# A decoder layer on one core: query stacks read part by part from a scratch in the stack's order, the residual sum as its own GpSimd step, and a new step order

## The chip, the cores and the metric

The kernel runs on one core of a Trainium2 chip. TensorE (PE) multiplies matrices into the eight banks of PSUM, VectorE (DVE) and ScalarE (ACT) read PSUM and SBUF, GpSimd (POOL) works on SBUF, and SyncE (SP) issues every DMA here. The metric is the device time of one execution in microseconds, the median of three runs.

## What is computed

One decoder layer on x (4 batches, 512 rows, 128 features), all in float32:

```
x = x + attn(layernorm(x))        # self attention by distances: softmax(-gamma * |xi - xj|^2) @ x
x = x + xattn(layernorm(x), ctx)  # 16 heads of 8 features over 154 context rows, with ALiBi slopes
x = x + ffn(layernorm(x))         # 8 experts of 128x128, the two best of each row, no weighting

scores = einsum('bhqd,bhkd->bhqk', q, k) / sqrt(dk) + slopes * (i - j)
attn   = softmax(scores, axis=-1)
```

## The kernel before

Each of the four batches b goes through the same steps. A step is written `name:b` or `name:b.k`, and each engine walks its own list of them in `ORDER` (line 44 on). The five lists are fixed tables, so an engine that meets a step whose semaphore is not yet there waits, and everything behind it in its list waits too. The tables stand for SP ("sync"), POOL ("gpsimd"), ACT ("scalar"), DVE ("vector") and PE ("tensor").

The steps of a batch in the order of the data:

- `stats1`, `rstd1`, `y1`, `y1T`: first layernorm (DVE statistics, POOL square root at L459, DVE normalising at L670) and its transpose through PE and ACT.
- `dist`, `rowmax`, `soft`, `probs`, `self`: distances as 512x512 matmuls (L913), row maxima on DVE (L687, L700), exponentials on ACT (L559), transposes of them, and the attention sum on PE (L932).
- `gather` (DVE, L710) adds the input and gives x1, with the statistics of the second layernorm; `rstd2` (POOL, L457 and L459), `y2` (DVE, L670), `y2T`.
- `query`: a matmul (L945), ACT's scaled copy into `qf` (L587), and a split into three bf16 parts `qpart`: the first by ACT, the second and third by DVE (L757 to L761). SP writes the parts to `q_scratch` in DRAM and reads them back as the stack `qs`, in which each head's 8 features stand six times in the order that the bf16 products need (`Q_PART`, 48 rows for each parity s of the head). Before the change SP waits for all three writes and then reads 48 rows of 8 pieces of 1 KB for each s. The key stacks `kA` and `kB` are made alike from `k_scratch`, once for each batch.
- `maxima` (PE L973, DVE L768): the largest score of each row and head, 22 groups of up to three heads through the two banks `MX`. It needs `qs` and `kA`. `mcat`, `mT`: the 64 maxima of a row, transposed, go through `m_scratch` in DRAM into six rows of `qs`.
- `scores` (PE L999 and L1003, ACT exponentials L611) needs `kB` and those six rows; `values` (L1019, L1023), `divide`, `aoT`, `wo` (L1050), with x2 from DVE (L801).
- x1 plus the output bias is `x1b`, which `wo` adds. It is made on POOL at the end of `rstd2` (L521), right behind the square root.
- `y3`, `y3T`, `route` (L1061), `mask`, then for each expert `spread` (PE L1083), `select` (DVE L848), `experts` (PE L1096); `fT`, `store`.

`WARM` (L117) puts matmuls on constant data (L870) ahead of certain steps; they compute nothing that is used. There are 91 of them in the program. Keys are prepared in the first batch: `keys:0` is two ACT copies (L572), four DVE instructions (L732 to L738), and DMAs that SP issues.

## Time and profile before

| | |
|---|---|
| median of 3 runs | 244.94 us (243.94 to 246.68) |
| the profiled execution | 244.3 us |
| its span | 242.5 us |
| PE matmuls busy | 206.0 us, 85% |
| DVE busy | 157.9 us, 65% |
| ACT busy | 109.2 us, 45% |
| POOL busy | 36.7 us, 15% |
| DMA traffic | 16.91 MB |

The span runs from the first to the last instruction; the time of the execution has 1.8 us more around it. Matmul busy time counts the matmuls on constant data as well, and a busy share is a mean over stages with different limits, so the stages are read one by one.

### The profile page before, as it was taken

The page shows a single profiled execution, that of the slowest core. Times are in us where ns is not written, and L with a number is a line of the kernel's source. Part 1 is how long each engine was busy: PE and PEld are TensorE (multiplying, and loading weights), DVE is VectorE, ACT ScalarE, POOL GpSimd, SP SyncE. Part 2 cuts the span into 40 slices and gives each one's busy share as a digit, 9 for nine tenths or more (in the row PEclk, how much of TensorE's full clock was granted, in tenths as well). Part 3 has the DMA queues.
Part 4 walks back from the last instruction along what each step waited for, and adds up shares of the span by engine and source line. Part 5 has one row for each costly group of instructions (what it writes and reads, how often), then busy time and mean ns, then how long its engine had stood idle before and what let it go on. Part 6 is the DMA issues. An engine that isn't in the chain of part 4 may idle for free.

```text
span 242.5 us, 3528 instructions
## 1 busy us (share of the span) xinstructions
PE 206.0 (85%) x1206; PEld 104.7 (43%) x1224; DVE 157.9 (65%) x433; ACT 109.2 (45%) x206; POOL 36.7 (15%) x98
## 2 busy tenths in 40 slices
PE   7488956878958898998999999889987878899994
PEld 2247622436612234474353457643333342335573
DVE  2476536499662488847686699776589513479772
ACT  2286053730317476828635566276133137821300
POOL 5604184300130030005000000130000001002000
PEclk9999999999975999999999999999999979999999
DMA  6997504900204500120152021203601010000011
GB/s 170 310 265 259 110 1 158 223 4 0 57 0 144 119 1 0 41 59 0 68 142 53 0 45 43 58 3 131 130 0 40 11 51 0 0 4 0 1 46 43
DMA packets 23031, 16.91 MB, mean 70 GB/s; under 512 B 10548, under 2 KB 21644, under 8 KB 22924
## 3 DMA queue, kind: packets, MB, share of 16 engines
q1 hardware_dynamic: 23012, 16.67, 26.8%
q8 instruction: 10, 0.16, 0.3%
q14 instruction: 9, 0.07, 0.1%
HBM read 11.29 MB, written 5.37 MB: 69 GB/s over the span
## 4 chain that ended last, share of the span: by engine, by line
PE 50%; DVE 24%; ACT 9%; issue 7%; POOL 4%; DMA 3%; another core or an unknown queue 1%; SPq 0%; ACTq 0%; DVEq 0%; POOLq 0%
DVE nm L768 12%; PE bank L1096 11%; PE bank L875 6%; PE bank L932 5%; PE bank L1023 4%; PE bank L913 4%; PE bank L973 3%; PE bank L1083 3%; DVE y L670 3%; PE bank L1003 3%; POOL rs L459 3%; PE bank L1019 2%; PE bank L870 2%; ACT w L551 2%; DVE x L710 2%
## 5 line engine op out<-in xcount | busy, mean ns | idle before, releaser
L768 DVE TENSOR_REDUCE nm<-bank 128x3 f32<-128x462 f32 x88 | 49.4, 618 | 10.9 <-PE bank L973 10.7
L611 ACT ACTIVATE pt<-bank 128x512 f32<-128x512 f32 x64 | 34.7, 597 | 22.9 <-PE bank L1003 15.2
L973 PE MATMUL bank<-kA,qs 128*128 128x308 bf16 (+1 forms) x172 | 29.2, 264 | 6.5 <-DVE nm L768 5.3
L1096 PE MATMUL bank<-ym,ewT 128*128 128x512 f32 (+1 forms) x80 | 32.5, 511 | 0.3 <-DVE ym L848 0.3
L848 DVE TENSOR_TENSOR ym<-bank,y3T 128x512 f32<-128x512 f32 (+1 forms) x40 | 22.1, 579 | 8.2 <-PE bank L1083 6.8
L870 PE MATMUL bank<-idle 128*128 128x512 bf16 x82 | 22.9, 406 | 3.3 <-DVE idle L655 1.5
L457 POOL TENSOR_SCALAR ve<-mv 128x4 f32<-128x4 f32 (+1 forms) x13 | 2.6, 198 | 151.4 <-DVE mv L663 151.1
L973 PEld LDWEIGHTS bank<-kA,qs 128*128 128x128 bf16 x172 | 12.1, 97 | 28.5 <-DVE nm L768 24.0
L1003 PE MATMUL bank<-qs,kB 128*128 128x512 bf16 x59 | 20.5, 397 | 3.4 <-ACT ptail L611 1.2
L913 PE MATMUL bank<-y1Tg,y1T 128*128 128x512 f32 x32 | 17.9, 641 | 5.5 <-ACT w L551 4.4
L551 ACT ACTIVATE w<-bank,snsq,sgn 128x512 f32<-128x512 f32 x16 | 12.3, 773 | 16.0 <-DVE rm L687 16.0
L687 DVE TENSOR_REDUCE rm<-bank 128x1 f32<-128x512 f32 x16 | 10.9, 688 | 12.6 <-PE bank L914 12.6
L1023 PE MATMUL bank<-pt,vm 128*32 128x512 f32 x128 | 16.9, 598 | 0.3 <-issue 0.3
L670 DVE TENSOR_SCALAR y<-x,mv,rs 128x128 f32<-128x128 f32 x32 | 11.3, 425 | 8.1 <-POOL rs L459 8.0
L1096 PEld LDWEIGHTS bank<-ym,ewT 128*128 128x128 f32 x80 | 13.6, 190 | 5.1 <-DVE ym L848 1.8
L932 PE MATMUL bank<-y,pT 128*128 128x128 f32 x128 | 15.3, 278 | 0.2 <-ACT pT L535 0.2
L870 PEld LDWEIGHTS bank<-idle 128*128 128x128 bf16 x91 | 8.9, 102 | 14.8 <-issue 2.4
L932 PEld LDWEIGHTS bank<-y,pT 128*128 128x128 f32 x128 | 14.6, 192 | 0.6 <-ACT pT L535 0.4
L875 PE MATMUL bank<-ident,y 128*128 128x128 f32 x48 | 7.7, 280 | 6.9 <-DVE y L670 6.9
L559 ACT ACTIVATE w<-w,nrb,sgn 128x512 f32<-128x512 f32 x16 | 12.9, 811 | 1.0 <-DVE nrb L700 0.6
L459 POOL TENSOR_TENSOR rs<-ve,minus_half 128x4 f32<-128x4 f32 (+1 forms) x13 | 13.2, 1012 | 1.1
L1003 PEld LDWEIGHTS bank<-qs,kB 128*128 128x128 bf16 x64 | 6.2, 101 | 14.1 <-ACT pt L611 7.4
(130 smaller groups left out, 275.3 us busy)
## 6 DMA issues: line engine op xcount, KB each, us to landing
qs<-q_scratch SPq DMA_DIRECT2D x8, 384.0 KB, 4.9
q_scratch<-qpart SPq DMA_DIRECT2D x4, 384.0 KB, 2.4
xs<-in_x_dram SPq DMA_DIRECT2D x4, 256.0 KB, 7.2
vm<-in_vm_ones_dram SPq DMA_DIRECT2D x1, 1024.0 KB, 12.0
q_scratch<-qpart SPq DMA_DIRECT2D x4, 256.0 KB, 2.1
kA<-k_scratch SPq DMA_DIRECT2D x8, 120.0 KB, 2.7
kB<-k_scratch SPq DMA_DIRECT2D x8, 120.0 KB, 2.6
out_dram<-ob SPq DMA_DIRECT2D x3, 256.0 KB, 2.4
```

The source lines that it names most:

```text
L459: g.tensor_tensor(rs[:, at], ve[:, at], minus_half[:, at], ALU.pow).then_inc(rstd[i], 1)
L611: nc.scalar.activation(dst, ST[n % 2][:, :], ACT.Exp).then_inc(exps, 1)
L768: v.tensor_reduce(negated[:, GROUP * g:GROUP * g + heads], MX[n % 2][:, 0:heads * J].rearrange("p (s j) -> p s j", s=heads), AX.X, ALU.max ...
L848: v.tensor_tensor(ym[:, e, at], MX[n % 2][:, at], y3T[:, at], ALU.mult).then_inc(mx_free, 1)
L870: mm(bank_[:, :], idle[:, 0:P], idle[:, :], start=True, stop=True)
L875: last = nc.tensor.transpose(bank_[:, tile(t)], src(t), id_[:, :])
L913: mm((A0S, A1S)[t % 2][b][:, :], y1T[:, tile(t)], y1Tg[:, :], start=True, stop=False)
L932: last = mm(A0S[b][:, tile(t)], pT[:, b % 2, t, u, :], y1[:, b % 2, u, :], start=(u == 0), stop=(u == T - 1))
L973: last = mm(MX[n % 2][:, at * J:(at + heads) * J], qs[:, b % 2, a, tile(t)], kA[:, s:s + heads, a, 0:J], start=True, stop=True)
L1003: last = mm(ST[n % 2][:, :], kB[:, h % 2, h // 2, 0:JM], qs[:, b % 2, h // 2, :], start=True, stop=True)
L1023: last = mm(YV[32 * g:32 * g + 32, :], vm[:, b, R * g + k, :], pt[:, (G * k + g) % PT_RING, :], start=False, stop=(k % 2 == 1), skip_group ...
L1096: last = mm(YMS[b][p][:, at], ewT[:, e, :], ym[:, e, at], start=False, stop=(e == E - 1))
```

## The change

Four things are edited.

1. The rows of Wq and Wk are permuted on the way in (`order`), so that a partition of q and k is (parity s, feature c, pair a). The scratches become `[2, COPY, HALF, ...]`, laid out as the stacks are. A row of a stack is then one contiguous piece (8 KB for `qs`, 2,560 bytes for a key stack).
2. Each write of a part is two DMAs of 64 partitions instead of one of 128, each part has a semaphore of its own, and `qs` is read in six DMAs (24, 16 and 8 rows for each s), each pair behind its own part's write. Key writes are twice as many DMAs as well.
3. `x1b` becomes a step `residual` that waits for the third part of the query (`q_lo`) and stands at another place in POOL's list.
4. All five lists of `ORDER` are replaced, and so is `WARM`: 63 matmuls on constant data instead of 91.

```diff
-        k_scratch = nc.dram_tensor("k_scratch", [B, P, COPY, JP], BF16, kind="Internal").ap()
-        q_scratch = nc.dram_tensor("q_scratch", [P, COPY, S], BF16, kind="Internal").ap()
+        k_scratch = nc.dram_tensor("k_scratch", [B, 2, COPY, HALF, JP], BF16, kind="Internal").ap()
+        q_scratch = nc.dram_tensor("q_scratch", [2, COPY, HALF, S], BF16, kind="Internal").ap()
...
             def query(b, _):
+                if b >= 1:
+                    sp.wait_ge(qs_in, 6 * ONE * b)
                 for part, (got, (r, n)) in enumerate(zip((q_hi, q_mid, q_lo), RUNS)):
                     sp.wait_ge(got, b + 1)
-                    load(q_scratch[:, r:r + n, :], qpart[:, part, :].unsqueeze(1).broadcast_to([P, n, S]), q_out)
+                    for s in range(2):
+                        load(q_scratch[s, r:r + n].rearrange("k p n -> p k n"),
+                             qpart[s * HALF:(s + 1) * HALF, part, :].unsqueeze(1).broadcast_to([HALF, n, S]), q_out[part])
...
-                sp.wait_ge(q_out, 3 * ONE * (b + 1))
-                for s in range(2):
-                    load(qs[s * ROWS:(s + 1) * ROWS, b % 2, :, :],
-                         q_scratch.rearrange("(a s c) k n -> s (c k) a n", s=2, c=DK)[s], qs_in)
+                for part, (r, n) in enumerate(RUNS):
+                    sp.wait_ge(q_out[part], 2 * ONE * (b + 1))
+                    for s in range(2):
+                        load(qs[s * ROWS + r * DK:s * ROWS + (r + n) * DK, b % 2, :, :],
+                             q_scratch[s, r:r + n].rearrange("k (c a) n -> (k c) a n", c=DK), qs_in)
...
             def rstd2(b, _):
                 norm(1, b, mv2, ve2, rs2)
+
+            def residual(b, _):
+                pool.wait_ge(q_lo, b + 1)
                 if b == 0:
                     pool.wait_ge(weights_in, W_LOADS * ONE)
...
-    order = np.arange(D)
+    order = np.arange(D).reshape(PAIRS, 2, DK).transpose(1, 2, 0).reshape(D)
```

The list of POOL and the constants of `WARM`, before and after:

```diff
-        rstd1:0 rstd1:1 rstd2:0 weights:0 rstd1:2 rstd2:1 rstd1:3 rstd2:2 rstd3:0 rstd3:1 rstd2:3 rstd3:2
-        rstd3:3.0 rstd3:3.1
+        rstd1:0 rstd1:1 rstd2:0 weights:0 rstd1:2 residual:0 rstd2:1 rstd1:3 residual:1 rstd3:0 rstd2:2 rstd3:1
+        residual:2 rstd2:3 residual:3 rstd3:2 rstd3:3.0 rstd3:3.1
...
-    "y1T:0": 14, "probs:0": 1, "y1T:1": 9, "y2T:0": 9, "query:0": 2, "probs:1": 16, "maxima:0": 1, "y2T:1": 16,
-    "query:1": 2, "scores:0": 1, "scores:1": 2, "y2T:2": 3, "wo:1.0": 1, "y3T:1.0": 2, "scores:2": 2, "y2T:3": 2,
-    "query:3": 1, "maxima:3": 1, "divide:2.1": 3, "spread:3.0": 3,
+    "y1T:0": 16, "probs:0": 1, "y2T:0": 10, "query:0": 1, "probs:1": 6, "y1T:2": 6, "y2T:1": 5, "query:1": 4,
+    "scores:0": 2, "divide:0.1": 2, "scores:1": 1, "scores:2": 6, "spread:3.0": 3,
```

The lines of the file shift by up to 11, so a row of before at L973 stands at L984 in the changed kernel. Three places show what moves.

DVE in the first batch, from the second layernorm of batch 0 (`y<-x`) to the first maxima (`nm<-bank`), before:

```order
L670 TENSOR_SCALAR y<-x,mv,rs 128x128 x4
L757 TENSOR_TENSOR qr<-qf,qpart 128x512
L759 CAST qpart<-qr 128x512
L761 TENSOR_TENSOR qpart<-qr,qpart 128x512
L687 TENSOR_REDUCE rm<-bank 128x1 x4
L670 TENSOR_SCALAR y<-xs,mv,rs 128x128 x4
L697 SCALAR_TENSOR_TENSOR rma<-rm,sgn,snsq 128x4
L700 TENSOR_SCALAR nrb<-rma,nsgn 128x4
L768 TENSOR_REDUCE nm<-bank 128x3 x21
```

and now:

```order
L681 TENSOR_SCALAR y<-x,mv,rs 128x128 x4
L768 TENSOR_TENSOR qr<-qf,qpart 128x512
L770 CAST qpart<-qr 128x512
L772 TENSOR_TENSOR qpart<-qr,qpart 128x512
L698 TENSOR_REDUCE rm<-bank 128x1 x4
L708 SCALAR_TENSOR_TENSOR rma<-rm,sgn,snsq 128x4
L711 TENSOR_SCALAR nrb<-rma,nsgn 128x4
L681 TENSOR_SCALAR y<-xs,mv,rs 128x128 x4
L779 TENSOR_REDUCE nm<-bank 128x3 x21
```

The first layernorm of batch 2 (`y<-xs`) has moved from ahead of the row maxima of batch 1 (`rma`, `nrb`) to behind them.

PE just ahead of the maxima of the last batch (`kA,qs`), with the last experts of batch 1 (`ym,ewT`), its scores (`qs,kB`) and values (`pt,vm`) of batch 2, before:

```order
L1003 MATMUL bank<-qs,kB 128x512 x2
L1083 MATMUL bank<-maskT,spread 128x512
L1023 MATMUL bank<-pt,vm 32x512 x4
L1096 MATMUL bank<-ym,ewT 128x512 x2
L870 MATMUL bank<-idle 128x512
L973 MATMUL bank<-kA,qs 128x308
L973 MATMUL bank<-kA,qs 128x154 x2
L973 MATMUL bank<-kA,qs 128x308
L1096 MATMUL bank<-ym,ewT 128x512
```

and now:

```order
L1107 MATMUL bank<-ym,ewT 128x512 x2
L1094 MATMUL bank<-maskT,spread 128x512
L1014 MATMUL bank<-qs,kB 128x512 x2
L1107 MATMUL bank<-ym,ewT 128x512
L984 MATMUL bank<-kA,qs 128x308
L984 MATMUL bank<-kA,qs 128x154 x2
L984 MATMUL bank<-kA,qs 128x308
L1034 MATMUL bank<-pt,vm 32x512 x4
L984 MATMUL bank<-kA,qs 128x308
```

The second half of the values, `values:2.1`, now stands behind the first maxima, and of the experts two (`experts:1.6` and `1.7`) stand behind the last of them, where `mT:3` follows.

SP around the query of batch 1, before:

```order
L346 DMA qs<-m_scratch 6x4096
L346 DMA q_scratch<-qpart 128x3x512
L346 DMA q_scratch<-qpart 128x2x512
L346 DMA q_scratch<-qpart 128x512
L346 DMA qs<-q_scratch 48x8x512 x2
L346 DMA kB<-k_scratch 48x8x160 x2
```

and now:

```order
L346 DMA qs<-m_scratch 6x4096
L346 DMA q_scratch<-qpart 64x3x512 x2
L346 DMA q_scratch<-qpart 64x2x512 x2
L346 DMA q_scratch<-qpart 64x512 x2
L346 DMA qs<-q_scratch 24x4096 x2
L346 DMA qs<-q_scratch 16x4096 x2
L346 DMA qs<-q_scratch 8x4096 x2
L346 DMA kB<-k_scratch 48x1280 x2
```

Twelve DMAs take the place of five, and a read's row is 4096 elements in one piece.

## Rows read from the trace of the kernel before

**Rows 1.** Page: busy us, share, count of each engine; TensorE's clock, 40 slices.
```profile
PE 206.0 (85%) x1206; PEld 104.7 (43%) x1224; DVE 157.9 (65%) x433; ACT 109.2 (45%) x206; POOL 36.7 (15%) x98
PEclk9999999999975999999999999999999979999999
```
**Rows 2.** Stretches: length, busy us of PE, PEld, DVE, ACT, POOL; clock, DMA, GB/s.
```profile
59.00:84.30 25.30, 20.70 (x97) 9.30 (x102) 13.03 (x49) 10.22 (x18) 3.59 (x5) 0.80 0.30 76
107.00:131.50 24.50, 21.95 (x118) 9.77 (x120) 17.78 (x50) 13.72 (x25) 3.48 (x5) 1.00 0.30 74
131.50:155.30 23.80, 23.29 (x163) 14.72 (x164) 19.34 (x48) 13.32 (x26) 1.20 (x2) 1.00 0.11 28
155.30:176.00 20.70, 18.76 (x99) 7.72 (x101) 13.50 (x35) 10.38 (x19) 2.26 (x3) 1.00 0.37 88
176.00:188.40 12.40, 10.14 (x61) 4.35 (x64) 11.72 (x21) 4.23 (x8) 0.00 (x0) 1.00 0.09 20
188.40:196.20 7.80, 5.67 (x47) 2.26 (x50) 3.49 (x11) 1.78 (x3) 0.00 (x0) 0.98 0.18 48
```
**Rows 3.** The same of L870 alone, the matmuls on constant data (PE, weight loads).
```profile
107.00:131.50 24.50, 1.19 (x4) 0.49 (x5) 1.00 0.30 74
155.30:176.00 20.70, 1.84 (x6) 0.58 (x6) 1.00 0.37 88
188.40:196.20 7.80, 0.59 (x2) 0.21 (x3) 0.98 0.18 48
```
**Rows 4.** Timeline of DVE: start, us, operation [idle before, releaser].
```profile
30.48 2.05 DVE L670 TENSOR_SCALAR y<-x,mv,rs 128x128 f32<-128x128 f32 x4 [1.50 <-POOL rs L459]
37.99 0.69 DVE L761 TENSOR_TENSOR qpart<-qr,qpart 128x512 bf16<-128x512 f32 x1
43.21 1.11 DVE L670 TENSOR_SCALAR y<-xs,mv,rs 128x128 f32<-128x128 f32 x4
...
66.83 1.82 DVE L670 TENSOR_SCALAR y<-x,mv,rs 128x128 f32<-128x128 f32 x4 [1.50 <-POOL rs L459]
```
**Rows 5.** Timeline of POOL at the first residual sum.
```profile
30.34 1.09 POOL L521 TENSOR_TENSOR x1b<-x,cols 128x512 f32<-128x512 f32 x1
```
**Rows 6.** Timeline of ACT: key copies, and around the exponentials of batch 1.
```profile
19.39 0.90 ACT L572 ACTIVATE kf<-bank,cols 128x308 f32<-128x308 f32 x2
...
43.33 0.78 ACT L551 ACTIVATE w<-bank,snsq,sgn 128x512 f32<-128x512 f32 x1 [0.30 <-DVE rm L687]
44.75 0.81 ACT L559 ACTIVATE w<-w,nrb,sgn 128x512 f32<-128x512 f32 x1 [0.64 <-DVE nrb L700]
```
**Rows 7.** Chain that ended last, in order of time: start, us, what.
```profile
47.60 10.19 DVE nm L768 x18
...
179.04 9.07 DVE nm L768 x16
...
191.24 2.04 DMA m_scratch<-mT
193.30 2.54 DMA qs<-m_scratch
```
**Rows 8.** Timeline of SP: the issues of the first query, writes and reads.
```profile
36.69 2.36 SPq L346 DMA_DIRECT2D q_scratch<-qpart  x3
40.48 0.83 SPq L346 DMA_DIRECT2D qs<-q_scratch  x2
```
**Rows 9.** DMAs from 36 to 50 us: landing of qs's reads; third write.
```profile
DMA to landing us min/median/max: 4.6/5.1/5.6
...
q_scratch<-qpart SPq DMA_DIRECT2D x1, 128.0 KB, 1.7
```
**Rows 10.** PE in the stretch at the lower clock.
```profile
69.00:80.00 11.00, 9.32 (x32) 2.43 (x31) 3.58 (x13) 6.26 (x11) 0.27 (x1) 0.53 0.36 107
```
**Rows 11.** Timeline of PE: the first matmuls behind two waits of about 2 us.
```profile
40.15 1.12 PE L913 MATMUL bank<-y1Tg,y1T 128*128 128x512 f32 x2 [2.25 <-ACT w L551]
...
68.71 0.66 PE L875 MATMUL bank<-ident,y 128*128 128x128 f32 x4 [2.02 <-DVE y L670]
```

More of the change, by code:

```diff
@@ L62 @@
[L62 to L65 removed]
+        y1T:0 dist:0.0 dist:0.1 soft:0.0 soft:0.1 dist:0.2 soft:0.2 dist:0.3 soft:0.3 probs:0.0 probs:0.1
+        probs:0.2 keys:0 probs:0.3 y1T:1 y2T:0 query:0 dist:1 soft:1.0 soft:1.1 probs:1.0 probs:1.1 soft:1.2
@@ L91 @@
-        scores:0.7 maxima:1.7 scores:0.8 maxima:1.8 divide:0.0 scores:0.9 maxima:1.9 values:0.2 maxima:1.10
-        values:0.3 probs:2.2 probs:2.3 divide:0.1 mT:1 self:2 aoT:0 scores:1.0 wo:0 scores:1.1 scores:1.2
-        scores:1.3 y2T:2 scores:1.4 y3T:0 query:2 route:0 scores:1.5 values:1.0 mask:0 values:1.1 spread:0.0
-        spread:0.1 y1T:3 spread:0.2 experts:0.0 spread:0.3 spread:0.4 experts:0.1 spread:0.5 experts:0.2
-        spread:0.6 spread:0.7 dist:3 maxima:2.0 experts:0.3 experts:0.4 maxima:2.1 scores:1.6 experts:0.5
@@ new lines @@
+        maxima:0.7 probs:1.3 maxima:0.8 maxima:0.9 maxima:0.10 self:1 y1T:2 mT:0 y2T:1 query:1 scores:0.0
+        scores:0.1 scores:0.2 scores:0.3 dist:2 scores:0.4 maxima:1.0 values:0.0 maxima:1.1 scores:0.5
+        maxima:1.2 scores:0.6 maxima:1.3 probs:2.0 scores:0.7 maxima:1.4 values:0.1 maxima:1.5 scores:0.8
+        maxima:1.6 divide:0.0 maxima:1.7 probs:2.1 scores:0.9 maxima:1.8 values:0.2 maxima:1.9 values:0.3
+        maxima:1.10 divide:0.1 probs:2.2 probs:2.3 aoT:0 mT:1 wo:0 self:2 scores:1.0 y3T:0 scores:1.1 route:0
@@ new lines @@
+        scores:1.2 scores:1.3 values:1.0 mask:0 y2T:2 scores:1.4 spread:0.0 spread:0.1 query:2 spread:0.2
+        scores:1.5 spread:0.3 experts:0.0 experts:0.1 spread:0.4 spread:0.5 y1T:3 experts:0.2 experts:0.3
+        spread:0.6 spread:0.7 dist:3 maxima:2.0 experts:0.4 experts:0.5 maxima:2.1 experts:0.6 experts:0.7
+        maxima:2.2 scores:1.6 fT:0 maxima:2.3 scores:1.7 values:1.1 maxima:2.4 scores:1.8 divide:1.0 maxima:2.5
+        scores:1.9 values:1.2 maxima:2.6 values:1.3 maxima:2.7 probs:3.0 divide:1.1 probs:3.1 maxima:2.8 aoT:1
@@ new lines @@
+        probs:3.2 maxima:2.9 wo:1 maxima:2.10 probs:3.3 self:3 mT:2 y3T:1 route:1 scores:2.0 mask:1 y2T:3
+        scores:2.1 spread:1.0 query:3 spread:1.1 spread:1.2 experts:1.0 scores:2.2 spread:1.3 experts:1.1
+        scores:2.3 experts:1.2 spread:1.4 spread:1.5 values:2.0 spread:1.6 scores:2.4 experts:1.3 experts:1.4
+        spread:1.7 scores:2.5 experts:1.5 maxima:3.0 values:2.1 maxima:3.1 scores:2.6 maxima:3.2 maxima:3.3
+        scores:2.7 maxima:3.4 maxima:3.5 maxima:3.6 scores:2.8 maxima:3.7 maxima:3.8 maxima:3.9 scores:2.9
@@ L584, in query @@
                 if b >= 1:
-                    act.wait_ge(q_out, 3 * ONE * b)
+                    for part in range(3):
+                        act.wait_ge(q_out[part], 2 * ONE * b)
                     act.wait_ge(q_lo, b)
```

103 lines of the change are left out of this document (47 added, 56 removed).

## The prediction, made before the changed kernel ran

> **What bounds the kernel now.** I read the page first, then the chain that ended last, then the engines' busy time in stretches between the steps, and last the timelines where an engine waits. The page [rows 1] shows matmuls on PE for 85% of the span, constant ones (L870) among them, and the clock line shows two weak places. The chain [rows 7] says what the page cannot: for 10.19 us behind 47.60 and 9.07 us behind 179.04 it lies on DVE's maxima (L768), near the end on the round trip of the maxima through DRAM, and elsewhere mostly on PE. So there are three kinds of stretches. From 131.5 to 155.3 PE is busy 23.29 of 23.80 us [rows 2]: there an order can gain almost nothing. From 176 to 188.4 DVE sets the pace. And ahead of the first maxima (26 to 47.6 us), from 59 to 84.3, and from 155.3 to 196.2, the path runs through a single batch's chain (normalise, query, DRAM, maxima), with PE waiting or running constant matmuls. That is where this change can act.
>
> **The DRAM round trip of the query.** In the first batch the third part is ready at 38.68 (37.99 + 0.69) [rows 4]. SP's issues of the writes end at 39.05, the third lands after 1.7 us [rows 9], the reads go out from 40.48 in 0.83 us for two [rows 8], and the later lands 5.6 us after its issue at about 40.8 [rows 9], so at 46.4: 7.7 us behind the third part. Now SP issues eight DMAs behind the third part (two writes, six reads) at 0.42 us each, by the pair of reads. The last issue starts 7 x 0.42 = 2.9 us behind it; the first two parts are already in DRAM by then. For the landing of the last read, of 64 KB in 8 KB rows, the nearest row is the read of `m_scratch`, which has 8 KB rows too, 2.54 us [rows 7]; the other end is today's 5.6 us. I take 2.6, since the last pair carries a sixth of the bytes: 5.5 us in all, against 7.7, and 8.5 at the worst end. The trip is 2.2 us shorter, or 0.8 longer.
>
> The Trainium skill ("DMA: Bandwidth & Descriptors", section "Why a DMA increments its semaphore by 16 and not by 1") says that a DMA runs on the largest number of engines up to 16 that divides its slowest dimension: 24, 16 and 8 rows would get 12, 16 and 8 engines where 48 rows have 16. By that the trip would shorten less or not at all. No row here shows the number of engines of a DMA.
>
> **Up to the first maxima, 3.2 us.** (a) The two key copies on ACT, 0.90 us at 19.39 [rows 6], stood ahead of all four copies of the first probabilities; three of these now go first. The attention sum can start after three, so it starts about 0.7 us earlier. Nothing takes this back: the key parts on DVE end about 2 us later than now, and their DMAs have until the maxima. (b) y2 takes 2.05 us while x1b (L521) runs beside it on POOL from 30.34, and 1.82 us in batch 1, where the same four instructions take 1.11 us with POOL idle [rows 4, 5, 6]. x1b now comes later, but in this batch POOL's `weights` follows in its place; I count 0.5 of the 0.94. (c) ACT's copies of y1T now come before those of y2T instead of between y2T and the query's copy: 0.3. So the third part is ready 1.5 us earlier, at 37.2. (d) The first exponential of batch 1 started at 44.75 and waited 0.64 us for DVE [rows 6], which had 1.11 us of y1:2 in front of the row maxima [rows 4]; that is now behind them. The relu copies end at 44.1 - 1.5 = 42.6 and the exponential follows at once, to 43.4. Transposes (0.45) and the first group bring the maxima to 44.4 instead of 47.6 [rows 7]: 3.2 us. The stack lands at 37.2 + 5.5 = 42.7, in time; at the worst end it lands at 45.7 and 1.5 us of the gain are lost. Ten fewer constant matmuls at probs:1 cost nothing: they filled this wait.
>
> **The second query, 0.4 us.** y2:1 gains 0.7 of its 1.82, but mT now stands ahead of y1T:2 on ACT, and with three copies behind it y2T:1 starts 0.3 late. The values' bias sums (2.3 us on DVE) move from behind y2:1 to ahead of gather:1, where the attention sum is still running.
>
> **The middle, 84.3 to 155.3, 1.0 us.** Idle time and constant matmuls are 24.50 - 21.95 + 1.19 = 3.7 us from 107 to 131.5, and about 0.7 from 131.5 to 155.3 [rows 2, 3]. The stack of batch 1 lands well ahead of its maxima. Every order has the same useful matmuls here, so between 0 and 3.7 can be won; I take 1.0, since the new order fills some waits with experts but pushes `self:2` behind `wo:0`.
>
> **From 155.3 to 196.2, 3.2 us.** Idle time and constant matmuls are 3.8 + 2.3 + 2.7 = 8.8 of 40.9 us (each length less busy plus L870's share) [rows 2, 3]; useful are 32.1. The stack of batch 3, 2.2 us earlier, lets the maxima start earlier, and the order fits: two experts and `values:2.1` (1.7 and 0.9 us) go behind the first maxima. What stays: six constant matmuls (1.3), unfilled waits (1.0), waits inside the maxima, where 22 groups at 9.07/16 = 0.57 us are a floor of 12.5 (1.5), and the wait for the maxima's trip, 2.04 + 2.54 us [rows 7], less what PE has to do meanwhile (1.8). That is 5.6 instead of 8.8 us. Here lies a new cost too: residual:2 follows rstd3:1 on POOL, so x1b runs beside y3:1 instead of y2:3, which moves 0.7 us and saves none in that batch. `stats1:3` now waits on SP ahead of the kB loads of batch 2; they come later than now, behind the last maxima of batch 2, but still ahead of mT:2's trip, which the scores need as well, so at no cost.
>
> The Trainium skill ("SBUF — State Buffer", section "Who interferes with whom") says that the port pair of VectorE and GpSimd is an exclusive lock for a whole instruction, against VectorE's two-port modes, and never against a reduction. By that the later x1b is free beside the maxima of batches 0 and 1 and costs the 0.7 us beside y3:1.
>
> **The rest, 0.4 us.** Two constant matmuls and a small wait ahead of the last values. The tail behind 216 us keeps its work.
>
> **Sum:** 3.2 + 0.4 + 1.0 + 3.2 + 0.4 = 8.2 us off the profiled execution's 244.3: 236.1. The median of the runs shown is 0.6 above that execution, so 236.7; I say 236.5. The terms' ends are 1.7 to 3.7, 0 to 1, 0 to 3.7, 0.5 to 4.5 and 0 to 1.
>
> **Rivals.** (1) *The gain of the front is not passed on*: a wait in the crowded lists of the later batches, or one more stretch at the lower clock, takes back the last three terms. Left are 3.2 + 0.4: 241. For it speaks the stretch at 131.5, where PE has no slack; against it the 8.8 us further on. (2) *The trip gets no shorter*, since twelve issues replace five and a read of 8 rows cannot use the whole DMA side: 0.8 us lost ahead of the first maxima and 1.8 in batch 3: 5.6 left, 239. This is the rival of the skill's rule on engines. (3) *The clock stays full.* From 69 to 80 us it was granted at 0.53 of 2.4 GHz, so for nearly all of it at its lower level of 1.2 GHz, after PE had been idle for 2.02 us [rows 11] and busy only in pieces, with 9.32 us of matmuls [rows 10]; I put what the full level would save at a third of these, 3 us, since matmuls double in their columns alone. If PE gets through there, 233.5. (4) *Slower*: the 28 constant matmuls that are gone held the clock. If PE falls to 1.2 GHz in the waits of all three other queries and of mT:3 too, at 3 us each, 12 us are lost and 8.2 won: 248.5. It decides from three such stretches beyond today's; one costs only rival 1. Against it speaks that a wait of 2.25 us at 40.15 [rows 11] left the clock line at its nines [rows 1], and that the new order shortens those waits.
>
> **How the numbers follow.** Chances: forecast 0.50 (its own range 234 to 239), rival 1 0.20, rival 2 0.12, rival 3 0.12, rival 4 0.06. The range from 232.0 to 241.5 leaves out rival 4, part of rival 1, and a full clock together with full terms. A measurement of this kernel tells 1% (2.4 us) from no change. Above 242.5 lie a third of rival 1 and a little of rival 2, within 1%; above 247.4 most of rival 4. Faster 0.86, same 0.09, slower 0.05.
>
> **What would show it.** The first group of maxima at 44 to 45 us; the reads of qs landed within 6 us of the third part; y2 of batches 1 and 3 at 1.1 us and y3:1 at 1.8; the maxima of the last batch starting at about 168 us instead of 176, and the scores of batch 3 at 188 to 189 instead of 196. I am wrong if the reads land later than 8 us after the third part, if PE's clock line shows more than two weak places, or if PE idles longer behind 84 us than now.

## The result and the profile after

The change made the kernel slower: 257.8 us (median of 4 runs, 256.54 to 258.4) against 245.69 us (243.94 to 246.68) before, a ratio of 1.049 [1.042, 1.057]. I had forecast 236.5 us and given "slower" 5 in 100. The profiled execution took 257.5 us with a span of 255.7 us. All ratios in this document, with their 95% intervals in brackets, leave out executions that were over 1.5% longer than the fastest of their kernel, at a lower granted clock; the medians take all.

The page of the changed kernel, PE's busy line and the clock line, answers [rows 1]:

```profile
PE 208.2 (81%) x1181; PEld 107.3 (42%) x1196; DVE 157.4 (62%) x433; ACT 109.9 (43%) x206; POOL 35.2 (14%) x98
...
PEclk9999999675999889997998899959988999999999
```

PE is busy for 2.2 us more although 28 constant matmuls are gone, and the clock line, with two weak places before, now has weak places in every part of the program. The reason stands in the chain that ended last (start, us, what), here its steps on the query's reads, on the last maxima and on their trip:

```profile
40.70 6.38 DMA qs<-q_scratch
...
81.96 6.35 DMA qs<-q_scratch
...
133.42 6.13 DMA qs<-q_scratch
...
183.37 5.63 DMA qs<-q_scratch
...
193.52 9.08 DVE nm L779 x16
...
207.21 2.64 DMA qs<-m_scratch
```

Before, the chain of [rows 7] had DVE's maxima at 179.04. They now stand at 193.52, as fast as then (9.08 against 9.07 us), and in all four batches the chain runs through the reads that the change was to shorten. Next the timelines of the changed kernel: DVE with y2 and the third part of the first batch, SP with its issues of writes and reads, and PE with the first group of maxima of each batch:

```profile
29.26 1.27 DVE L681 TENSOR_SCALAR y<-x,mv,rs 128x128 f32<-128x128 f32 x4 [0.33 <-POOL rs L466]
...
35.92 0.69 DVE L772 TENSOR_TENSOR qpart<-qr,qpart 128x512 bf16<-128x512 f32 x1
```
```profile
34.46 3.98 SPq L346 DMA_DIRECT2D q_scratch<-qpart  x6
38.54 2.45 SPq L346 DMA_DIRECT2D qs<-q_scratch  x6
```
```profile
47.22 0.93 PE L984 MATMUL bank<-kA,qs 128*128 128x308 bf16 x4 [3.67 <-DMA qs<-q_scratch]
...
88.55 0.93 PE L984 MATMUL bank<-kA,qs 128*128 128x308 bf16 x4 [3.20 <-DMA qs<-q_scratch]
...
139.80 0.93 PE L984 MATMUL bank<-kA,qs 128*128 128x308 bf16 x4 [3.50 <-DMA qs<-q_scratch]
...
189.34 0.56 PE L984 MATMUL bank<-kA,qs 128*128 128x308 bf16 x4 [3.74 <-DMA qs<-q_scratch]
```

The third part is ready at 36.61 (35.92 + 0.69), 2.1 us earlier than in [rows 4]. The maxima start at 47.22, when PE started them at 47.20 before. I call the time from the third part to the first maxima the trip: it takes 10.6 us, 10.5 of them to the landing of the reads (40.70 + 6.38 = 47.08), where [rows 8, 9] gave 7.7 to the landing. PE stands idle for over 3 us in each batch, and in three batches of four the first four matmuls behind that wait take 0.93 us, in the last 0.56. The stretches of the changed kernel (columns as in [rows 2]), from the start of one batch's maxima on:

```profile
47.20:66.70 19.50, 16.78 (x87) 11.08 (x89) 14.85 (x35) 3.38 (x7) 0.00 (x0) 0.66 0.14 34
...
139.80:163.50 23.70, 23.57 (x162) 14.57 (x163) 17.94 (x42) 12.29 (x24) 1.91 (x3) 0.94 0.01 3
163.50:189.90 26.40, 20.71 (x102) 9.40 (x106) 14.52 (x41) 10.00 (x18) 2.64 (x4) 0.87 0.32 81
189.90:203.00 13.10, 10.60 (x55) 4.02 (x57) 11.69 (x21) 4.69 (x9) 0.00 (x0) 0.87 0.00 0
```

From 47.2 to 66.7 the granted clock is 0.66 of 2.4 GHz, between its two levels and so for most of the stretch at 1.2 GHz. The three last stretches, at 0.94, 0.87 and 0.87, answer those of [rows 2] that stood at 1.00.

### The profile page after: what moved, and what is told of

It reads as the page before. It is cut to its first block, busy times and chain, and to the rows that moved or that the text cites. A ratio compares the mean times of both kernels' runs of the same rounds, so it can differ in the third digit from the quotient of the medians.

```text
span 255.7 us, 3526 instructions
## 1 busy us (share of the span) xinstructions
PE 208.2 (81%) x1181; PEld 107.3 (42%) x1196; DVE 157.4 (62%) x433; ACT 109.9 (43%) x206; POOL 35.2 (14%) x98
## 4 chain that ended last, share of the span: by engine, by line
PE 42%; DVE 19%; DMA 14%; ACT 8%; SPq 8%; issue 6%; POOL 2%; ACTq 0%; DVEq 0%; POOLq 0%
DMA qs<-q_scratch 10%; DVE nm L779 8%; SPq L346 8%; PE bank L886 7%; PE bank L984 6%; PE bank L1107 6%; PE bank L1034 5%; PE bank L943 3%; PE bank L1030 3%; PE bank L1014 3%; DVE ym L859 2%; DVE y L681 2%; PE bank L956 2%; PE bank L1072 2%; DVE st L671 1%
## 5 line engine op out<-in xcount | busy, mean ns | idle before, releaser
L984 PE MATMUL bank<-kA,qs 128*128 128x308 bf16 (+1 forms) x172 | 32.4, 298 | 20.0 <-DMA qs<-q_scratch 14.1
L984 PEld LDWEIGHTS bank<-kA,qs 128*128 128x128 bf16 x172 | 13.9, 106 | 45.1 <-DVE nm L779 24.6
L1014 PE MATMUL bank<-qs,kB 128*128 128x512 bf16 x57 | 19.2, 394 | 3.4 <-ACT pt L622 1.8
L924 PE MATMUL bank<-y1Tg,y1T 128*128 128x512 f32 x32 | 16.9, 610 | 5.2 <-ACT w L561 4.4
L881 PE MATMUL bank<-idle 128*128 128x512 bf16 x57 | 17.4, 448 | 3.2 <-DVE idle L666 1.5
L1034 PE MATMUL bank<-pt,vm 128*32 128x512 f32 x128 | 18.0, 637 | 0.0
L698 DVE TENSOR_REDUCE rm<-bank 128x1 f32<-128x512 f32 x16 | 10.9, 689 | 10.4 <-PE bank L925 10.4
L943 PEld LDWEIGHTS bank<-y,pT 128*128 128x128 f32 x128 | 15.6, 203 | 0.4 <-ACT pT L545 0.4
L545 ACT ACTIVATE pT<-bank 128x512 f32<-128x512 f32 x16 | 9.3, 595 | 15.1 <-PE bank L886 15.1
L622 ACT ACTIVATE ptail<-bank 128x512 f32<-128x512 f32 x16 | 8.7, 596 | 11.9 <-PE bank L1010 11.9
L886 PE MATMUL bank<-ident,w 128*128 128x128 f32 x64 | 10.7, 304 | 1.1 <-ACT pT L545 0.5
```

The costliest lines, as they stand in the source:

```text
L622: nc.scalar.activation(dst, ST[n % 2][:, :], ACT.Exp).then_inc(exps, 1)
L881: mm(bank_[:, :], idle[:, 0:P], idle[:, :], start=True, stop=True)
L886: last = nc.tensor.transpose(bank_[:, tile(t)], src(t), id_[:, :])
L924: mm((A0S, A1S)[t % 2][b][:, :], y1T[:, tile(t)], y1Tg[:, :], start=True, stop=False)
L943: last = mm(A0S[b][:, tile(t)], pT[:, b % 2, t, u, :], y1[:, b % 2, u, :], start=(u == 0), stop=(u == T - 1))
L984: last = mm(MX[n % 2][:, at * J:(at + heads) * J], qs[:, b % 2, a, tile(t)], kA[:, s:s + heads, a, 0:J], start=True, stop=True)
```

## The experiments

Three theories stood against each other at first: the new reads are slow because 24, 16 and 8 rows get few DMA engines (A); they are slow because of their 8 KB rows (B); the new order itself costs, with 28 fewer constant matmuls, and the trip only shows it (C). Each experiment ran beside runs of the kernel before, whose medians were 243.6 to 244.4 us. The ratios below are to these.

**The order alone.** Kernel before, its DMAs and layout untouched, with the `residual` step, `ORDER` and `WARM` of the changed kernel.

> The kernel before with all of its DMAs, scratch layouts and permutation, but with the residual step, the five lists and the constants of the changed one. Theories A and B (the trip is what costs): the trip is 7 to 8 us again, the maxima of batch 0 start near 45 us, and the time is 238 to 244 us, my forecast without its shorter trip (239) being in it. Theory C (the order, with 28 fewer constant matmuls, costs): 250 us or more, with weak places in the clock line although the trip is short.

**237.6 us**, ratio 0.974 [0.964, 0.984]: faster by 6.7 us, and theory C falls. Its page, and the starts of its first and last maxima and of the scores of batch 3 on PE:

```profile
PE 197.0 (84%) x1196; PEld 100.7 (43%) x1196; DVE 156.5 (67%) x433; ACT 109.7 (47%) x206; POOL 35.9 (15%) x98
...
PEclk9999999999999999999999999999999999999999
```
```profile
44.18 0.56 PE L975 MATMUL bank<-kA,qs 128*128 128x308 bf16 x4 [0.92 <-DMA qs<-q_scratch]
...
168.56 0.56 PE L975 MATMUL bank<-kA,qs 128*128 128x308 bf16 x4 [0.52 <-DMA qs<-q_scratch]
...
187.97 0.61 PE L1001 MATMUL bank<-qs,kB 128*32 128x512 bf16 x8 [0.94 <-DMA qs<-m_scratch]
```

In this execution the same lists with the same 63 constant matmuls hold PE's clock at full level throughout, with a trip of 7.8 us (36.34 to 44.18). PE is busy 11.2 us less than in the changed kernel for the same work. This execution was the fastest of e3's four (235.4 us); the other three took 237.6 to 237.9 us at a mean clock of 0.983 to 0.986. The same kernel with DMAs behind its end (e12) had its clock low for about 10 us between 48 and 62 us. So the full clock is the best case of e3, and not assured by its order.

**The DMAs alone.** Changed kernel with the lists, `WARM` and the place of `x1b` from before.

> The changed scratches, permutation, writes and six reads, but the lists, the constants and the place of x1b of the kernel before. Theories A and B: the trip is 10.5 to 11 us instead of 7.7, the maxima start about 3 us late in each of four batches, and the time is 251 to 257. Theory C: 244 to 248, as before, since the longer trip is hidden.

251.5 us, ratio 1.032 [1.021, 1.043]; the trip in batch 0 is 10.3 us (40.35 to 50.63). So the new DMAs cost 7 us in the old order and 20 us in the new one (257.8 less 237.6). The new order is worth 6.7 us with the short trip and costs 6 with the long one: the two parts of the change are not additive.

**Two reads instead of six, and 1 KB pieces instead of 8 KB rows.** Both on the changed kernel.

```diff
# e1_two_reads, behind the writes of all three parts
+                for s in range(2):
+                    load(qs[s * ROWS:(s + 1) * ROWS, b % 2, :, :],
+                         q_scratch[s].rearrange("k (c a) n -> (k c) a n", c=DK), qs_in)
# e2_pieces
+        q_scratch = nc.dram_tensor("q_scratch", [2, COPY, HALF, S + 32], BF16, kind="Internal").ap()[:, :, :, 0:S]
```

> The changed kernel, but qs is read by one DMA of 48 rows for each s (two instead of six), behind the writes of all three parts. Rows stay 8 KB in one piece; lists, constants and writes stay those of the changed kernel, in which the maxima started 10.6 to 11.3 us behind the third part and always waited last for the reads. Theory A (reads of 24, 16 and 8 rows have too few DMA engines): the trip falls to 8 us or less, the clock's weak places ahead of and behind the maxima shrink, and 257.8 us falls by 8 to 12, to 246 to 250. Theory B (the contiguous 8 KB rows are what is slow, on however many engines): the trip stays within 1 us of 10.6 and the time at 255 to 258. Theory C (the new order is to blame, the trip only shows it): 255 to 258 too, with a shorter trip.

> The changed kernel, but each 512-element line of q_scratch is followed by 32 unused elements, so a row of qs is again 8 pieces of 1 KB; the six reads, writes, lists and constants stay. Theory A (few engines for 24, 16 and 8 rows): the same bytes on as few engines, trip 10 to 12 us, time 256 to 260. Theory B (8 KB pieces are slow): trip 8 us or less, time 246 to 250. If both were at work, a trip in between.

Two reads: 249.2 us, ratio 1.025 [1.014, 1.037], trip 9.5 us. Pieces: 256.4 us, ratio 1.049 [1.036, 1.063], trip 10.9 us. Row size makes no difference that shows (256.4 against 257.8 us, 10.9 against 10.6), and the split of the reads does. But the two reads leave 1.7 us of the longer trip, which my text had not named.

**Sixteen rows for each read, and whole writes.** To get writes of 128 partitions with 8 KB rows, the scratch was laid out as copy, partition, column.

```diff
# e5_sixteen_rows
+                for k, part in ((0, 0), (2, 1), (4, 2)):
+                    sp.wait_ge(q_out[part], 2 * ONE * (b + 1))
+                    for s in range(2):
+                        load(qs[s * ROWS + k * DK:s * ROWS + (k + 2) * DK, b % 2, :, :],
+                             q_scratch[s, k:k + 2].rearrange("k (c a) n -> (k c) a n", c=DK), qs_in)
# e8_three_writes (two reads) and e9_three_writes_sixteen (the six reads of e5)
+        q_scratch = nc.dram_tensor("q_scratch", [COPY, P, S], BF16, kind="Internal").ap()
...
+                         q_scratch[:, s * HALF:(s + 1) * HALF].rearrange("k (c a) n -> k c (a n)", c=DK), qs_in)
```

> The changed kernel, still with six reads and six writes, but the reads take 16 rows each (copies 0 and 1, 2 and 3, 4 and 5 of the stack, behind parts 1, 2 and 3) instead of 24, 16 and 8. Theory A (24 and 8 rows use too few DMA engines, 16 rows use all): no read is on few engines, so the rate while they run rises from about 125 GB/s to 190 to 270, and although the last pair now carries a third of the bytes, the maxima start 8 to 9.5 us behind the third part instead of 10.6 to 11.3; time 247 to 251, about that of the two reads of 48 rows (249.2) or better. Theory A' (what costs is six small reads behind one another, whatever their rows): trip 10.5 to 11.5, time 255 to 259.

> The two reads of 48 rows (249.2 us), and the scratch laid out as copy, partition, column, so that each part is again one write of 128 partitions: five issues instead of eight, rows still 8 KB in one piece. Theory D (what is left of the longer trip after the repair of the reads is the twelve, here eight, issues on SP, of which the pairs of writes cost 1.5 us): reads issued 1.5 us earlier, trip 7.7 to 8.2, time 240 to 244. Theory B (8 KB pieces have a price of their own): trip 9 us or more and 246 to 249.

> Both repairs, and still part by part: three writes of 128 partitions and six reads of 16 rows, each pair behind its part. If theories A and D hold, this is the trip that the change was written for: a third of the bytes behind the last part, 6 to 7.5 us, maxima of batch 0 at 43 to 44 us, time 235 to 240. If part-by-part reading gains nothing on this path, 240 to 246, no better than the two reads.

255.2 us (1.046 [1.040, 1.051]), 257.6 us (1.059 [1.054, 1.064]) and 287.6 us (1.181 [1.177, 1.186]). e5 came out as theory A' said: no read has fewer than 16 rows, and the trip is still 10.5 us, so theory A in its simple form does not carry the loss. The times of e8 and e9 missed every value that I had written down. In e8 and e9 I had changed more than I meant to: the outermost dimension of a read's source is now the copy, of size 6 and 2. First of e8, then of e9: the chain's step on the first batch's reads (start, us), and the DMA lines (GB/s in 40 slices, for e9 also the busy tenths of the 16 engines) of a later batch's reads, from 82 to 91 us and from 144 to 163 us:

```profile
40.20 8.18 DMA qs<-q_scratch
```
```profile
GB/s 73 146 0 36 109 146 146 109 182 73 109 146 109 146 182 36 109 73 109 109 182 146 109 218 146 146 109 146 73 73 36 0 0 0 0 0 0 0 0 0
```
```profile
40.23 14.12 DMA qs<-q_scratch
```
```profile
DMA  0002001011111111111111011111111111110000
GB/s 26 17 0 34 0 34 52 34 52 52 52 52 69 52 52 52 52 52 52 52 52 69 34 69 52 52 52 52 52 52 52 52 69 52 52 52 0 0 0 0
```

With an outer dimension of 2 the reads run at a nearly even 52 GB/s with 10 to 20% of the 16 engines' time busy; if that is two engines, each moves 26 GB/s. With 6 the slices lie mostly between 73 and 182. That is the rule of the Trainium skill ("DMA: Bandwidth & Descriptors", section "Why a DMA increments its semaphore by 16 and not by 1"), that the slowest dimension sets the number of engines, and here the trace agrees. A limit of 2 or 6 engines is met in these two kernels alone.

**Constants into the waits.** Ten constant matmuls ahead of the maxima of each batch in the changed kernel; six, four, six and six in the kernel with two reads.

```diff
# e6_constants; e14_two_reads_constants has 6, 4, 6, 6
+    "maxima:0": 10, "maxima:1": 10, "maxima:2": 10, "maxima:3": 10,
```

> The changed kernel with ten more matmuls on constant data ahead of the maxima of every batch, into the wait of 3.2 to 3.7 us for the reads (ten take about 3 us at the full clock), so the reads are as late as in the changed kernel but PE does not stand idle for them. Theory E (a large part of the loss is the clock that falls behind each wait, PE being busy 208.2 us where the same list takes 197.0 at the full clock): 249 to 253, a granted clock of 0.97 or more, the groups of maxima of batch 0 in 12.4 us instead of 15.1. If the clock costs little beside the waits themselves: 255 to 258.

> The two reads of 48 rows (249.2 us, trip 9.5 to 10.4) with six, four, six and six matmuls on constant data in the waits ahead of the maxima. By theory E the clock's share of what is left is recovered: the waits of 1.7 to 3.3 us stay as they are, but the clock line keeps its nines, 241 to 245. If the remaining loss is only late data: 247 to 249.

250.2 us (1.025 [1.018, 1.032]) and 245.1 us (1.003 [0.999, 1.008]), so 7.6 us come back against the changed kernel and 4.1 against the kernel with two reads, although the data arrives hardly sooner: the trips in e6 are 10.5 to 10.9 us, and the four of e14 take 38.8 us where e1's took 39.9. The stretch of the maxima of batch 0, changed kernel and then e6 (columns as in [rows 2]):

```profile
47.20:57.00 9.80, 7.83 (x38) 4.31 (x38) 7.80 (x14) 2.78 (x6) 0.00 (x0) 0.67 0.19 40
```
```profile
49.80:59.00 9.20, 6.68 (x46) 3.50 (x46) 8.83 (x16) 2.78 (x6) 0.00 (x0) 1.00 0.22 47
```

46 matmuls take 6.68 us at the full clock, 38 take 7.83 at 0.67; the maxima's own take 265 ns each in the one and 341 in the other.

**A longer trip and nothing else.** The new order with the old DMAs (e3), plus one DMA of 1 KB and its wait between the query's writes and reads.

```diff
# e10_longer_trip
+                load(pause[b], qpart[0:16, 2, 0:32], paused)
+                sp.wait_ge(paused, ONE * (b + 1))
```

> The kernel with the new order and the old DMAs (237.6 us), and one small DMA of 1 KB with its wait put between the query's writes and its reads on SP: the trip grows by about 2.3 us (0.4 to issue, 1.7 to 2 to land), to 10.1 us from 7.8, near the 10.6 to 11.3 of the changed kernel, and nothing else changes. Theory F (the length of the trip alone, with the clock that falls in the longer waits, explains the changed kernel's loss of 20 us): well over 4 x 2.3 = 9.2 us, at 249 to 256, with several weak places in the clock line. If the waits cost only their length: 245 to 247. If something else in the changed DMAs (keys, 64-partition writes beside other work) is at fault: 240 to 244, the rest being hidden.

248.1 us, ratio 1.017 [1.012, 1.023]: 10.4 us lost against e3. SP's rows, PE's first maxima, and the seven us from about the start of the maxima of batches 0 and 1 on (columns as in [rows 2]):

```profile
38.31 0.33 SPq L346 DMA_DIRECT2D pause<-qpart  x1
39.63 0.83 SPq L346 DMA_DIRECT2D qs<-q_scratch  x2
```
```profile
45.42 0.55 PE L979 MATMUL bank<-kA,qs 128*128 128x308 bf16 x4 [1.98 <-DMA qs<-q_scratch]
```
```profile
45.00:52.00 7.00, 5.31 (x29) 2.94 (x30) 5.39 (x10) 2.78 (x6) 0.74 (x1) 0.76 0.44 82
82.00:89.00 7.00, 6.37 (x50) 2.91 (x54) 4.83 (x9) 4.30 (x10) 2.91 (x10) 1.00 0.01 2
```

The pause was shorter than I expected (1.3 us from issue to landing, the chain says), and the four trips grew by 6.4 us in all, from 32.6 to 39.0. The time is a little below the band for theory F, but the size per us fits it: 10.4 us for 6.4, while PE is busy 7.6 us more on the same matmuls. PE's waits ahead of the maxima are 1.98, 1.58, 3.01 and 2.75 us here, where e3 had 0.92, 0.01, 1.48 and 0.52. The granted clock is 0.76 in the seven us from the first, the third and the fourth start of the maxima on, and 1.00 from the second.

**The two halves of the longer trip.** On the kernel with the new order and the old DMAs: each part written by two DMAs of 64 partitions; or each s read by 24, 16 and 8 rows. And on the changed kernel, the reads of parts 1 and 2 issued ahead of the write, or right behind it, of the third.

```diff
# e15_half_writes
+                    for s in range(2):
+                        load(q_scratch[s * HALF:(s + 1) * HALF, r:r + n, :],
+                             qpart[s * HALF:(s + 1) * HALF, part, :].unsqueeze(1).broadcast_to([HALF, n, S]), q_out)
# e16_six_reads
+                for r, n in ((0, 24), (24, 16), (40, 8)):
+                    for s in range(2):
+                        load(qs[s * ROWS + r:s * ROWS + r + n, b % 2, :, :],
+                             q_scratch.rearrange("(a s c) k n -> s (c k) a n", s=2, c=DK)[s, r:r + n], qs_in)
# e13_read_between
+                    if part:
+                        read(b, part - 1)
+                read(b, 2)
```

> The new order with the old layout and the two old reads of 48 rows in 1 KB pieces (237.6 us), but each part is written by two DMAs of 64 partitions instead of one of 128, as in the changed kernel. By the DMAs measured alone (a write from 64 partitions takes as long as one of twice the bytes from 128) the 768 KB are written 1.3 us slower, and three more issues add 0.3 to 0.4: the trip is 9.3 to 9.6 us instead of 7.8, as with the changed kernel's two reads, and by about 7 us for each us of trip the time is 247 to 250, so the kernel with two reads of 8 KB rows (249.2) is explained by its writes alone, and neither row size nor the key DMAs have a part in it. If they have, 240 to 244.

> The new order, old layout and old writes of 128 partitions (237.6 us), but each s is read by DMAs of 24, 16 and 8 rows (1 KB pieces) instead of one of 48. If the split of the reads alone stretches their transfer from 4.1 to about 6 us, the trip is 9.3 to 10 us and the time 246 to 252. If six reads cost only behind halved writes, 238 to 241.

> The changed kernel, but SP issues the reads of part 1 between the writes of parts 2 and 3, and those of part 2 ahead of its last pair, so that reading really starts before the third part is ready. Theory G (the parts are ready within 2.2 us of each other and one write needs 2.1 to 2.8 us to land, so nothing can be read early): the last write is now held back by the wait for the first one, the trip stays at 10.5 us or grows to 12, 257 to 262. If reading early is what the change lacked: 9 us or less and 245 to 250.

Half writes: 249.3 us, ratio 1.013 [1.000, 1.025], from four runs that lie as far apart as 245.4 and 252.9 us; trip 9.6 us, about that of two reads of 8 KB rows (9.5). Six reads: 256.9 us, ratio 1.049 [1.034, 1.063], above the 246 to 252 expected; trip 10.1 us, as expected. Reads between the writes: 257.3 us, ratio 1.057 [1.048, 1.067], trip 10.3 us: no better than the changed kernel. SP's rows in the first batch, e3, then e15, then e16; behind those of e3 and e15 the chain's steps on the last write and the last read:

```profile
34.35 2.36 SPq L345 DMA_DIRECT2D q_scratch<-qpart  x3
38.13 0.84 SPq L345 DMA_DIRECT2D qs<-q_scratch  x2
```
```profile
36.37 1.70 DMA q_scratch<-qpart
38.49 5.55 DMA qs<-q_scratch
```
```profile
35.43 3.95 SPq L345 DMA_DIRECT2D q_scratch<-qpart  x6
40.91 0.82 SPq L345 DMA_DIRECT2D qs<-q_scratch  x2
```
```profile
38.78 2.06 DMA q_scratch<-qpart
41.26 5.56 DMA qs<-q_scratch
```
```profile
35.38 2.25 SPq L345 DMA_DIRECT2D q_scratch<-qpart  x3
39.06 2.36 SPq L345 DMA_DIRECT2D qs<-q_scratch  x6
```

Half writes put off the first read (3.6 us behind the third part instead of 1.8). Most of that is issuing: the last write goes out 1.46 us behind the third part (38.78 less 37.32) and not 0.03 (36.37 less 36.34), since six issues of about 0.6 us stand where three of 0.34 to 0.38 did; it then lands in 2.06 us instead of 1.70. The reads themselves take as long as in e3 (5.56 and 5.55 us for the last). Six reads leave the first where it was and stretch what follows: 8.3 us from first issue to first maxima instead of 6.05, of which 1.5 are the longer issuing.

In e13 nothing was read before the third part was ready either. The first part's write, issued at 36.36, had to land first, so the first read went out at 39.84, 1.3 us behind the third part (38.51), and the third part's writes at 40.60.

**DMAs measured alone.** One at a time, behind the end of e3.

> Behind the end of the kernel with the new order and old DMAs, 26 DMAs run one at a time, each waited for: reads of 8 KB rows with 48, 24, 16, 8 and 2 rows on neighbouring partitions, with 16 rows on every fourth and every eighth partition, and in 1 KB pieces, writes of 64 and of 128 partitions, and the old read of 48 rows in pieces. The total is about 90 us longer than the kernel. If the number of rows sets the number of DMA engines (26 GB/s for each, from the kernel whose reads ran at 52 GB/s): 2 rows are on 2 engines, 8 rows on 8, 24 rows on 12, and 24 rows land later than 16 by one packet. If it is where the rows lie in SBUF (packets took 309 ns where two to six were in flight and 968 with sixteen, all into 16 neighbouring partitions), 16 rows on every fourth or eighth partition land 0.6 us or more earlier than 16 neighbours, with packets of 309 to 600 ns; and a write from 64 partitions runs at about 200 GB/s where one from 128 runs at 300. If neither, all land at times proportional to their bytes.

One execution, span 318.8 us; the list of 13 DMAs ran twice. Behind the end of its issue SP waited for the landing of 48 rows 4.4 us (4.1 the second time) where they went to partitions 0 to 47, and 3.2 us (3.4) where they went to 48 to 95; 4.1 us (4.0) for the 48 rows of the old 1 KB pieces, 2.7 for 24 rows, 2.3 to 2.6 for 16, 2.2 for 8 and 1.8 for 2. So a read has about 1.8 us that no small size takes away, and reads of 24, 16 and 8 rows sum to more than one of 48. Sixteen rows on every fourth or eighth partition landed in 1.9 to 2.0 us, but their issues took 0.5 us instead of 0.3, so from the start of the issue they gain 0.1 to 0.5 us on neighbours, less than the 0.6 expected. Where the rows lie does matter for 48 of them: about 1 us between equal reads into different partitions. It matters for the writes too. DMA lines (busy tenths and GB/s, 40 slices) of the write from 64 partitions, 192 KB (271 to 273.6 us), and of the one from 128 partitions, 384 KB (273 to 276 us):

```profile
DMA  0000000000000004798898978998742000000000
GB/s 0 0 0 0 0 0 0 0 0 0 0 0 0 0 0 126 205 268 189 189 221 205 236 173 189 221 236 189 189 111 79 0 0 0 0 0 0 0 0 0
```
```profile
DMA  0000000000000000017999999999999620000000
GB/s 14 0 0 0 0 0 0 0 0 0 0 0 0 0 0 0 0 68 259 355 396 423 341 382 382 437 369 355 410 396 396 219 55 0 0 0 0 0 0 0
```

Sixteen slices of 0.065 us for 192 KB, sixteen of 0.075 us for 384 KB, and SP waited 2.1 us for either, behind an issue of 0.65 us for the half and 0.38 for the whole: half the partitions take nearly as long for half the bytes. The Trainium skill ("SBUF — State Buffer", section "Door 1: The DMA port swizzle") says that partitions 0 to 63 reach only 8 of the 16 ports by which DMAs get at SBUF; the trace agrees, with about 200 GB/s against 380. No run wrote from another set of 64 partitions alone. In e15, with writes from both halves in flight, single slices reach 380 GB/s, so there the slow half writes partly overlap.

**The place of x1b.** e3 with the sum back at the end of `rstd2`.

> The kernel with the new order and the old DMAs (237.6 us), but x1 plus bias is again made at the end of rstd2, beside y2. By my forecast's terms y2 takes 1.8 to 2.05 us again instead of 1.1 to 1.27, on the path in each batch, so 1 to 3 us slower: 238.5 to 240.5. If the place of this sum does not matter: 237 to 238.

239.3 us, ratio 0.983 [0.978, 0.988], against 0.974 [0.964, 0.984]: 1.6 us slower by the medians, but the intervals overlap. What is clear is the row on DVE, which is that of [rows 4] again, beside 1.27 in the changed kernel:

```profile
30.88 2.05 DVE L669 TENSOR_SCALAR y<-x,mv,rs 128x128 f32<-128x128 f32 x4 [0.33 <-POOL rs L458]
```

## The trip and the time, all runs together

Third part ready and first maxima from the timelines of DVE and PE, first read from SP's; then the four trips' sum, PE's busy time from the page, the time of that same execution, and the median. All rows use the new lists, the last two with more constants than the 63; e11 has the sum for x1b at its old place.

| kernel | batch 0: ready, first read, maxima | trip 0 | four trips | PE busy | this execution | median |
|---|---|---|---|---|---|---|
| e3 order only | 36.34, 38.13, 44.18 | 7.8 | 32.6 | 197.0 | 235.4 | 237.6 |
| e11 x1b back | 39.26, 41.04, 47.16 | 7.9 | 32.7 | 202.0 | 241.3 | 239.3 |
| e10 pause | 36.51, 39.63, 45.42 | 8.9 | 39.0 | 204.6 | 248.1 | 248.1 |
| e1 two reads | 38.02, 41.56, 47.48 | 9.5 | 39.9 | 206.0 | 248.5 | 249.2 |
| e15 half writes | 37.32, 40.91, 46.95 | 9.6 | 40.9 | 207.8 | 251.7 | 249.3 |
| e16 six reads | 37.26, 39.06, 47.32 | 10.1 | 42.5 | 207.7 | 253.5 | 256.9 |
| e5 sixteen rows | 38.29, 40.30, 48.80 | 10.5 | 43.0 | 209.3 | 256.8 | 255.2 |
| e13 reads between | 38.51, 39.84, 48.83 | 10.3 | 44.3 | 207.6 | 257.3 | 257.3 |
| e2 pieces | 36.53, 38.52, 47.38 | 10.9 | 45.1 | 204.5 | 253.7 | 256.4 |
| changed kernel | 36.61, 38.54, 47.22 | 10.6 | 43.8 | 208.2 | 257.5 | 257.8 |
| e8 outer 6 | 37.49, 39.31, 48.52 | 11.0 | 45.1 | 210.0 | 259.1 | 257.6 |
| e9 outer 2 | 36.35, 36.90, 54.49 | 18.1 | 74.7 | 207.2 | 287.4 | 287.6 |
| e14 two reads, with constants | 38.41, 41.82, 47.55 | 9.1 | 38.8 | 205.9 | 244.1 | 245.1 |
| e6 changed, with constants | 39.21, 41.33, 49.77 | 10.6 | 42.6 | 209.4 | 248.5 | 250.2 |

Against e3 the changed kernel's trips are 11.2 us longer in all, and its time is 20.2 us longer by the medians. Trips and PE's busy time belong to one execution, so what is left beyond the trips is best counted with that execution's own time: 22.1 us longer, of which 10.9 are not trips. In e9 it is 9.9 of 52.0, in e10 6.3 of 12.7. This rest does not go by the length of the trips: e2 has 5.8 us of it at 12.5 us of longer trips, e9 9.9 at 42.1. It goes by how much longer PE is busy on the same matmuls, and lies 0.3 to 3.2 us below that in every row with longer trips and the 63 constants (11.2 for the changed kernel, 10.2 for e9, 7.6 for e10, 7.5 for e2). With constants in the wait 3.1 us are left in e6 (248.5 less 235.4, less 10.0 of trips).

That a slower PE is the clock and not other work is shown by e6; that a us of clock loss costs a us of time everywhere is not, since some of it lies beside waits. And not all of the slower clock comes from the trip: e11's profiled execution has trips as short as e3's, yet PE is busy 5.0 us more and it took 5.9 us longer than e3's. Against e3's other three runs every rest is 2.2 to 2.6 us smaller.

## Why the prediction was wrong

**Where it held.** The order does what I worked out. With the trip left as it was, my rival 2 gave a gain of 5.6 us and 239; e3 gained 6.7 and took 237.6. Its landmarks are those of the forecast: first maxima at 44 to 45 (44.18), last at about 168 (168.56), scores of batch 3 at 188 to 189 (187.97). The third part was ready 2.1 us earlier instead of 1.5 in the changed kernel, though e1 and e5, with the same code up to there, had it 1.4 to 1.7 us later, only 0.4 to 0.7 us ahead of before; the size of this term is not settled. y2 took 1.27 and 1.11 us. One detail fell elsewhere: beside the moved x1b it was not y3:1 that got slower (1.10 us where I expected 1.8) but the subtraction just ahead of it, in the changed kernel's timelines of POOL and DVE:

```profile
162.75 1.09 POOL L531 TENSOR_TENSOR x1b<-x,cols 128x512 f32<-128x512 f32 x1
162.91 1.01 DVE L795 TENSOR_TENSOR mcat<-nmr,mcat 128x64 bf16<-128x64 f32 x1
...
163.85 1.10 DVE L681 TENSOR_SCALAR y<-x,mv,rs 128x128 f32<-128x128 f32 x4
```

The same instruction took 0.22 us in batch 0. The 0.8 us are a real price, near the 0.7 that I had put on y3:1: y3:1 starts behind it, and the chain that ended last passes there.

**The step that failed** is the landing of the reads: "I take 2.6, since the last pair carries a sixth of the bytes: 5.5 us in all, against 7.7, and 8.5 at the worst end." It was 10.5 to the landing and 10.6 to the first maxima. The last read was issued 4.1 us behind the third part instead of 2.9 and landed after 6.4 us instead of 2.6. Three things were wrong.

- *The bytes.* The last pair does carry a sixth, but nothing has been read by then: the code issues all six writes before the first read, at 38.54, 1.9 us behind the third part. So all 768 KB of reads pass behind it, as before, and in smaller pieces. The chain's last step takes 6.38 us where I had 2.6, and where even my worst end, the old landing, had 5.6. A row for the read of 48 KB (`m_scratch`, 2.54 us) was no neighbour of a read with 700 KB ahead of it.
- *The issues.* I counted 0.42 us for each of the eight issues behind the third part, the price of a read. The six reads did take that (2.45 us). A half write takes about 0.6 us to issue, 3.98 for the six with a short wait for the second part, and no row of before had such a write. When the third part was ready, SP was still issuing the second part's. The last read went out at 40.70, 4.1 us behind the third part; in this batch SP did not stand waiting for a write to land, in the last one it did (chain: the last write from 179.77 to 183.04, the last read at 183.37, 5.0 us behind the third part).
- *Half writes.* Apart from their number I gave them no price. Alone they take the trip from 7.8 to 9.6 us (e15), 1.4 of it through their issues and 0.4 through a slower landing of the last.

Against e3, whose last read was issued 2.2 us behind the third part and landed after 5.55, the trip of the changed kernel is 1.9 us longer by issuing and 0.8 by landing.

Reading part by part, ahead of the last write, brought nothing in the one order tried (e13): the parts become ready within 2.2 us of each other (first write issued at 34.46, third part at 36.61), and one half write takes 2.1 to 2.8 us to land. Whole writes with reads part by part are not tested: e9 was meant for that and failed by its layout. In batch 0 of e3 the first part's write landed 1.3 us ahead of the third's (34.35 + 2.4 against 36.37 + 1.70), and as an estimate that is the most it could gain.

**Rival 2** had the right place and the wrong depth: it let the trip grow by 0.8 us at most. The rule on engines beside it agrees with e8 and e9, and does not explain the cost here (e5).

**Rival 4** had the right mechanism of the loss beside the trip, PE falling to 1.2 GHz in the waits of every batch, and its 12 us were near the 9 (by the medians) to 11 (by the profiled executions) beyond the trips. That the size came so near is luck, for I tied it to the wrong cause. With the 28 constant matmuls gone and the old trip the clock is at 0.98 to 1.00 (e3), against 0.93 to 0.94 in the changed kernel. What pulled it down was the longer waits that the trip makes: 3.2 to 3.7 us ahead of the maxima here, and already 2.0 to 3.0 in e10. Since I took the waits to get shorter, I gave it 6 in 100. The two errors were one: the sign of the trip decided both terms, and I had put its chance of being longer by 2 us or more at nothing.

**The conditions for being wrong** were the right ones: reads later than 8 us behind the third part, more than two weak places in the clock line, PE idle longer behind 84 us. All three came.

What stays open is how the clock comes to fall in one execution and not in another of the same kernel. It makes e16's profiled execution 253.5 us (clock 0.953), which its 9.9 us of longer trips and PE's 10.7 us of longer work cover, and its other three 256.4 to 257.7 (0.927 to 0.933). Open too is whether the 24 half key writes, where there were twelve whole ones, cost anything. e1, which has them, and e15, which has not, have trips of 9.5 and 9.6 us and medians of 249.2 and 249.3, but e15's runs lie so far apart (245.4 to 252.9) that a cost of up to 3 us could hide there.

## What to carry to other kernels

When a DMA is split so that its data can follow in parts, price all bytes that still pass behind the last part and every issue with its own kind's row, and check in the code whether a read is issued before the last write at all. A change that lengthens waits on an engine whose clock falls in them costs more than the waits: here 20 us for 11 us of trips. And a change of several parts should be timed part by part: the order alone (237.6 us) beats both kernels, while with the new DMAs it makes the slowest pairing of the four.
